# A transformer layer in fp32 on one core: MLP output product in three split passes, heads in fewer transfers

## The reference

```python
qkv_in = rat_read(hidden, read_w ...)            # 3 mixes of width 512, each normalised
attn   = attention(qkv_in, qkv_w, pos)           # causal, rotary, [T, 512]
hidden = rat_write(hidden, attn, wod_w, wab_w ...)
g_in, u_in = split(rat_read(hidden, mlp_read_w ...))
mlp    = silu(g_in @ W0.T) * (u_in @ W1.T)       # [T, 2048]
hidden = rat_write(hidden, mlp, wod_w, wab_w ...)
x = x + hidden
x = x + ffn(layernorm(x))                        # router over 8 low-rank experts

def rat_write(res, y, ...):
    o_d = y @ wod_w.T                            # 512 columns out, 8 of "delta_low"
    A_B = y @ wab_w.T + wab_b                    # 112 columns of gates
    delta = softplus(delta_low @ du_w.T + du_b)
    ...                                          # A_full, B_full: elementwise from delta and the gates
    return hs * A_full + out * B_full
```

## Time and profile before

| | us |
|---|---|
| median of 3 runs | 1699.76 (1698.36 to 1703.68) |
| the profiled execution | 1699.55 |
| its span, first to last instruction | 1697.7 |
| TensorE busy | 1552.1 (91%) |
| VectorE busy | 1157.3 (68%) |
| ScalarE busy | 840.9 (50%) |
| GpSimd busy | 525.1 (31%) |
| DMA moved | 366.45 MB, mean 216 GB/s |

### The profile page before, as it was taken

How to read it: one execution, slowest core, us unless ns; L and a number is a source line. 1 busy time by engine, 2 the same in 40 slices (tenths; PEclk the granted TensorE clock), 3 DMA queues, 4 the chain that set the end, 5 groups by cost and what they waited for, 6 DMA issues and landing times.

```text
span 1697.7 us, 22468 instructions
## 1 busy us (share of the span) xinstructions
PE 1552.1 (91%) x8278; PEld 1052.8 (62%) x8278; DVE 1157.3 (68%) x1686; ACT 840.9 (50%) x1528; POOL 525.1 (31%) x430
## 2 busy tenths in 40 slices
PE   6999999999999977599998899988899989999976
PEld 5665555666666645577655677555677557876544
DVE  7777755888888857644458668767767874354775
ACT  5233235888888755444234456234465325442352
POOL 1424533333331000225563641452551352000000
PEclk9999999999999988699999999999999999999987
DMA  9657567888786155367675577766677766676743
GB/s 359 210 196 303 183 172 223 237 220 240 212 233 178 46 195 162 132 205 247 218 267 186 189 258 278 244 219 203 234 250 259 263 209 194 222 247 215 233 157 136
DMA packets 126273, 366.45 MB, mean 216 GB/s; under 512 B 16066, under 2 KB 33090, under 8 KB 110932
## 3 DMA queue, kind: packets, MB, share of 16 engines
q1 hardware_dynamic: 125876, 364.88, 66.1%
q10 hardware_dynamic: 288, 0.13, 0.0%
HBM read 289.20 MB, written 75.76 MB: 215 GB/s over the span
## 4 chain that ended last, share of the span: by engine, by line
PE 69%; DVE 17%; ACT 8%; issue 3%; DMA 2%; POOL 1%; SPq 0%; DVEq 0%; ACTq 0%
PE ps L1574 20%; PE ps L1586 11%; PE ps L545 6%; PE ps L1038 5%; PE ps L1025 4%; PE ps L1061 4%; PE ps L1544 3%; PE ps L1532 3%; ACT a_p L1140 3%; PE ps L1489 2%; DVE m_A L1644 2%; PE ps L504 2%; PE ps L1473 2%; PE ps L1504 1%; DMA p_x<-in_x 1%
## 5 line engine op out<-in xcount | busy, mean ns | idle before, releaser
L1574 PE MATMUL ps<-m_yhi,m_win 128*128 128x512 f32 x1024 | 355.9, 416 | 0.0
L1586 PE MATMUL ps<-m_wod,m_hT 128*128 128x512 f32 (+1 forms) x1024 | 296.8, 440 | 4.4 <-DVE m_mlp_ab L1779 2.5
L1586 PEld LDWEIGHTS ps<-m_wod,m_hT 128*128 128x128 f32 x1024 | 167.2, 194 | 147.1 <-issue 145.0
L1574 PEld LDWEIGHTS ps<-m_yhi,m_win 128*128 128x128 f32 x1024 | 195.1, 190 | 53.2 <-issue 8.2
L1082 DVE TENSOR_REDUCE a_negmax<-ps 128x1 f32<-128x640 f32 (+7 forms) x176 | 180.8, 1027 | 60.6 <-PE ps L1028 59.6
L1574 PE MATMUL ps<-m_ylo,m_win 128*128 128x512 f32 x512 | 204.0, 398 | 0.0
L1140 ACT ACTIVATE a_p<-ps,a_negmax 128x128 f32<-128x128 f32 (+7 forms) x256 | 188.8, 751 | 28.6 <-DVE a_negmax L1082 26.3
L1038 PE MATMUL ps<-ident,a_p 128*128 128x128 f32 x1152 | 156.7, 274 | 1.4 <-DVE a_pT L1095 1.2
L1964 POOL TENSOR_SCALAR e_moments<-e_moments 128x1 f32<-128x1 f32 x16 | 7.4, 463 | 431.5 <-ACT m_x L1875 401.5
L1025 PE MATMUL ps<-a_k,a_q 128*128 128x512 f32 (+3 forms) x384 | 123.5, 401 | 16.9 <-ACT a_p L1140 15.0
L1038 PEld LDWEIGHTS ps<-ident,a_p 128*128 128x128 f32 x1152 | 122.9, 141 | 3.3 <-DVE a_pT L1095 1.9
(11 more groups left out here) (218 smaller groups left out, 2808.9 us busy)
## 6 DMA issues: line engine op xcount, KB each, us to landing
m_win<-mlp_in_split SPq DMA_DIRECT2D x128, 512.0 KB, 4.5
m_wod<-in_wod2T SPq DMA_DIRECT2D x128, 316.0 KB, 3.4
m_wod<-in_wod1T SPq DMA_DIRECT2D x64, 316.0 KB, 3.6
p_xT<-in_xT SPq DMA_DIRECT2D x16, 1024.0 KB, 9.3
p_x<-in_x SPq DMA_DIRECT2D x16, 1024.0 KB, 10.6
a_q<-qk_split SPq DMA_DIRECT2D x64, 256.0 KB, 6.9
a_k<-qk_split SPq DMA_DIRECT2D x128, 128.0 KB, 7.1
mlp_in_split<-a_w_two SPq DMA_DIRECT2D x32, 512.0 KB, 3.5
```

Source lines behind the costliest of these rows:

```text
L1574: m = nc.tensor.matmul(bank_of("m", blk, step), win[s][:, wl, ic, :], y[:, k, :], start=(ic == 0 and p3 == 0), stop=(ic == HCH - 1 and p3 ...
L1586: m = nc.tensor.matmul(ps[:, b, 0:cn], hT[:, k, P * q:P * q + P], w2[s][:, c0:c0 + cn], start=(k == 0), stop=(k == MCH - 1))
```

## The change

1. Blocks 0 to 2 make the MLP output in fp32r, as the input products are made. The 632 columns are cut into two halves of 316 (`HALFW`); a half now covers all four tiles, with three products per tile and step: high x high, high x low, low x high. Each tile has one bank per half. Block 3 stays as it was, in fp32, two tiles per half.
2. `hT` is split on the chip: an entry `h` per chunk (16 per block), placed at steps 30.2 to 38.8, copies it into the high part on ScalarE and subtracts on VectorE for the low part. The high part uses the buffer of `yhi` and `ylo`; the next block's turns wait until the step that read it is done.
3. The MLP output weights are split by GpSimd beside attention: 32 more pieces of 316 columns; all 64 are spread evenly over units 0 to 163.
4. The heads: one transfer for q and two for k, each to two groups of partitions, instead of two and four; and one head per unit in units 2 to 5 instead of four in unit 3.
5. `PLACES` has new numbers throughout. The writes of a block's tiles, two of which began in the middle of the block, begin after it (w0 at 64 instead of 48). Buffers of the last four tiles are named anew.

```diff
+SPLIT = [blk < NBLK - 1 for blk in range(NBLK)]
+ROUNDS = [[(0, 1, 2, 3)] * 2 if SPLIT[blk] else [(0, 1), (2, 3)] for blk in range(NBLK)]
+HALFW = (H + 8 + 2 * 48 + 16) // 2
 PLACES = {...
-'A': 'loado': -3.11, 'wod': 1.56, 'low': 2, 'load': 3.17, 'delta': 4, 'gates': 5.65, 'scale': 7.94, 'sum': 9.57,
-     'piece0': 13.67, 'piece1': 13.68, 'piece2': 14.32, 'piece3': 14.5, 'stats': 18.05, 'norm': 20.16
+'A': 'loado': -1.0, 'wod': 1.09, 'low': 2.18, 'load': 4.08, 'delta': 4.24, 'gates': 6.17, 'scale': 8.72, 'sum': 9.72,
+     'piece0': 14.75, 'piece1': 14.76, 'piece2': 14.77, 'piece3': 16.73, 'stats': 18.62, 'norm': 20.12
-'FIRST': 'wod': 2.03, 'low': 3.03, 'delta': 4.35, 'gates': 5.03, 'scale': 6.03, 'sum': 7.29, ...
+'FIRST': 'wod': 0.95, 'low': 1.95, 'delta': 2.95, 'gates': 3.79, 'scale': 3.8, 'sum': 5.46, ...
-'a': 4: 0.0, 5: 12.0, 6: 24.0, 7: 36.05, 8: 50.7, 9: 66.7, 10: 81.09, 11: 98.7, 12: 114.7, ...
+'a': 4: -4.73, 5: 9.49, 6: 22.54, 7: 36.68, 8: 54.57, 9: 68.62, 10: 83.01, 11: 94.12, 12: 118.84, ...
-'w': 0: 48, 1: 64, 2: 81.06, 3: 96.37, 4: 112, 5: 127.33, 6: 144, 7: 160, 8: 176, 9: 192, 10: 208, 11: 224, ...
+'w': 0: 64, 1: 78.28, 2: 90.67, 3: 103.13, 4: 128.04, 5: 140, 6: 155, 7: 167.9, 8: 192.26, 9: 204, 10: 218.0, ...
-'t': first of block 1 62.25, of block 2 120.61, of block 3 185.15
+'t': first of block 1 56.81, of block 2 120.9, of block 3 183.25
+'h': 30.22, 30.72, 30.94, 31.22, 31.44, 32.5, 32.72, 32.73, 33.64, 33.73, 34.44, 35.24, 35.4, 37.1, 38.03, 38.83
...
+        placed += [(64 * blk + at, ("h", blk, "split", m)) for blk in range(NBLK) if SPLIT[blk]
+                   for m, at in enumerate(PLACES["h"])]
...
+            if SPLIT[blk]:
+                pe.wait_ge(hlo_ready, MCH * sum(SPLIT[:blk]) + k + 1)
+                for q in tiles:
+                    if k == 0:
+                        wait_for_bank(pe, "d", blk, q, r)
+                    for p3, (h, wl) in enumerate(((Y, 0), (Y, 1), (hT_lo, 0))):
+                        m = nc.tensor.matmul(bank_of("d", blk, q, r)[:, 0:HALFW], h[:, k, P * q:P * q + P],
+                                             w2s[s][:, wl, :], start=(k == 0 and p3 == 0),
+                                             stop=(k == MCH - 1 and p3 == 2))
...
+        def split_dve(blk, m):
+            dve.wait_ge(hhi_ready, MCH * sum(SPLIT[:blk]) + m + 1)
+            V.tensor_tensor(hT_lo[:, m, :], hT[:, m, :], Y[:, m, :].bitcast(F32), ALU.subtract).then_inc(hlo_ready, 1)
+        def split_act(blk, m):
+            act.wait_ge(mlp_mm, 32 * blk + (30 if m < MCH // 2 else 32))
+            wait_for_emptied(act, "m", blk, up_step(m))
+            S.activation(Y[:, m, :], hT[:, m, :], ACT.Copy).then_inc(hhi_ready, 1)
...
+            if blk and SPLIT[blk - 1]:
+                act.wait_ge(wod2_mm, wod2_done(blk - 1, 1, 2 * k + 1))
             wait_for_emptied(act, "t", blk, k)
+            S.activation(yhi[k], yraw[k % 2][:, :], ACT.Copy).then_inc(yhi_ready, 1)
...
+                for q in ROUNDS[blk][r]:
+                    act.wait_ge(wod2_mm, wod2_count[blk, r, k, q])
+                    act.wait_ge(hs_ready, nth("sum", *before_place(blk, q)))
...
+        PIECES = 4 * MCH
+        def pieces_at(n):
+            return [u for u in range(PIECES) if n == u * (NU - 10) // PIECES]
...
-            for r in range(2):
-                move(qs[s][64 * r:64 * r + 64, :], src_q).then_inc(slot_loaded[s], 16)
-            for r in range(4):
-                move(ks[s][32 * r:32 * r + 32, :], src_k[r // 2]).then_inc(slot_loaded[s], 16)
+            move(qs[s][:, :], src_q.unsqueeze(0).broadcast_to([2, 64, L])).then_inc(slot_loaded[s], 16)
+            for a in range(2):
+                move(ks[s][64 * a:64 * a + 64, :], src_k[a].unsqueeze(0).broadcast_to([2, 32, L])).then_inc(slot_loaded[s], 16)
...
-                if n < NU and si % 3 == 0 and u == 3 and sets[si][0] + 1 < fours:
+                if n < NU and si % 3 == 0 and u in (2, 3, 4, 5) and sets[si][0] + 1 < fours:
```

More of the change, by code:

```diff
@@ L47 @@
 ACT_SET = "natural_log_exp_and_others"
[L52 to L102, removed]
@@ new lines @@
+PLACES = {'A': {'loado': -1.0,
+       'wod': 1.09,
+       'low': 2.18,
+       'load': 4.08,
+       'delta': 4.24,
+       'gates': 6.17,
+       'scale': 8.72,
+       'sum': 9.72,
+       'piece0': 14.75,
+       'piece1': 14.76,
+       'piece2': 14.77,
+       'piece3': 16.73,
+       'stats': 18.62,
+       'norm': 20.12},
+ 'W': {'load': -0.7, 'low': 0, 'delta': 1.6, 'gates': 2.49, 'loadx': 3.3, 'scale': 3.87, 'sum': 5.21, 'x': 6.46},
+ 'E': {'mean': 8.55,
+       'turn0': 9.73,
+       'turn1': 10.69,
+       'spread': 12.86,
+       'down0': 13.14,
+       'turn2': 13.64,
+       'down1': 13.74,
+       'turn3': 14.21,
+       'down2': 15.46,
+       'down3': 15.58,
+       'router': 15.75,
+       'weigh': 16.93,
+       'lowT': 19.44,
+       'out0': 20.6,
+       'out1': 21.13,
+       'out2': 23.66,
+       'out3': 23.67,
+       'store': 23.68},
+ 'FIRST': {'loado': -102.01,
+           'load': -100.37,
+           'wod': 0.95,
+           'low': 1.95,
+           'delta': 2.95,
+           'gates': 3.79,
+           'scale': 3.8,
+           'sum': 5.46,
+           'turn0': 6.98,
+           'turn1': 6.99,
+           'turn2': 7.9,
+           'turn3': 7.91,
+           'read0': 8.59,
+           'read1': 8.6,
+           'read2': 10.8,
+           'read3': 10.81,
+           'stats': 11.86,
+           'norm': 13.35},
@@ L105 @@
        2: -194,
[L106 to L130, removed]
-       12: 240,
[L132 to L154, removed]
+       3: -191,
+       4: -4.73,
+       5: 9.49,
+       6: 22.54,
+       7: 36.68,
+       8: 54.57,
+       9: 68.62,
+       10: 83.01,
+       11: 94.12,
+       12: 118.84,
+       13: 132,
+       14: 145.3,
+       15: 159.5},
+ 'w': {0: 64,
+       1: 78.28,
+       2: 90.67,
+       3: 103.13,
+       4: 128.04,
+       5: 140,
+       6: 155,
+       7: 167.9,
+       8: 192.26,
+       9: 204,
+       10: 218.0,
+       11: 230.85,
+       12: 240,
+       13: 243.3,
+       14: 255.91,
+       15: 259.19},
+ 'e': {0: 64,
+       1: 78.48,
+       2: 91,
+       3: 103.35,
+       4: 129.61,
+       5: 143.11,
+       6: 155,
+       7: 171.01,
+       8: 192,
+       9: 203.89,
+       10: 223.5,
+       11: 231.08,
+       12: 239.56,
+       13: 245.5,
+       14: 254.71,
+       15: 260.67},
+ 't': [-2.97, -2.73, -2.49, -2.25, -2.01, -1.76, -1.52, -1.28, 56.81, 57.86, 58.91, 59.96, 61.01, 62.06, 63.11, 64.17,
+       120.9, 121.98, 123.05, 124.13, 125.2, 126.28, 127.36, 128.43, 183.25, 184.42, 185.59, 186.77, 187.94, 189.11,
+       190.29, 191.46],
+ 's': 36.83,
+ 'h': [30.22, 30.72, 30.94, 31.22, 31.44, 32.5, 32.72, 32.73, 33.64, 33.73, 34.44, 35.24, 35.4, 37.1, 38.03, 38.83]}
 class Engine:
@@ L1387, in program @@
             if what == "m" and part >= 32 and (part - 32) % MCH == 0:
-                for b in range(4):
-                    one.plan(("d", i, (part - 32) // MCH, b), b)
+                r = (part - 32) // MCH
+                for q2 in ROUNDS[i][r]:
+                    if SPLIT[i]:
+                        one.plan(("d", i, q2, r), q2, readers=1 + r)
+                    else:
+                        one.plan(("d", i, q2, 0), 2 * (q2 % 2))
+                        one.plan(("d", i, q2, 1), 2 * (q2 % 2) + 1)
             if what == "m" and (i, part) == (NBLK - 1, 63):
@@ L1793, in mix_dve @@
                     turn_dve(i, q)
+                elif what == "h":
+                    split_dve(i, q)
                 else:
```

150 lines of the change are left out of this document (94 added, 56 removed).

## The result

The changed kernel takes 2280.32 us (median of 4 runs, 2276.01 to 2283.72) against 1699.3 of the kernel before on the same chip: a ratio of 1.341 [1.338, 1.345]. 1666 us were predicted, 1640 to 1694 as the range. The prediction was wrong, in sign and by 614 us.

What follows compares the result with a forecast made beforehand. The prediction took TensorE (69% of the chain, the two MLP products longest), idling mostly for VectorE, as the bound. Terms -37+6+3-2-3 = -33 took the profiled 1699.55 us to 1666 us, range 1640 to 1694.

Steps and rivals of the forecast that it cites:

- Heads in 3 transfers: Attention stage: same bytes in 3 transfers instead of 6, no TensorE instruction waits there for a DMA: 0.
- 64 slices, one head at a time: Attention stage: GpSimd's pieces double to 64; heads are fetched early and backlog made up later: 0 (up to +33).
- Order of the mix stage: Writes, reads and turns around the MLP blocks: moved places priced only within small terms, part of +6, +3, -2, -3.
- +6: Blocks 1 and 2: subtractions raise VectorE to 82% busy, adding 3 us of TensorE idling to each (0 to +25).
- +3: Turn before block 1: TensorE waits 13 us on the late last attention write, in exchange for 11 us idled now.
- Output product with its splits: Blocks 0 to 2: 316-column products every 0.148 us, 1.78 us a step instead of 2.16: -37 us (bounds -73, +12).
- the rival of the weight loads: Output product: weight loads of 0.19 us set the pace of the narrow products; 1715 us, chance 0.06.
- VectorE takes over, 1684: Blocks 1 and 2: VectorE sustains no more than 78%, blocks take 251 and 232 us, +17 to +30; chance 0.14.
- Block 0: Block 1's first L1574 near 912 instead of 937: -12 products, -3 start, about 10 us of writes and experts leaving.
- The first writes: First four writes, before block 0: new order puts tile 0's scale ahead of the wait for tile 1's product: -3.
- The tail: After the last product: order much the same with two tiles a little earlier: -2 (-6 to +3).
- DMA engines: Attention: engines don't exceed a 0.84 share, so L1025 waits for a_q or a_k: +33, 1699 us, chance 0.05.

Runs made afterwards that it cites:

- after_heads6: Changed kernel with only the heads' transfers put back (q in two, k in four), still one head per unit: 1760.02 us, ratio 1.036.
- before_slices64: Kernel before with 64 weight slices split and stored instead of 32, the further 32 unused: 1727.25 us, ratio 1.015.
- heads6_group: Changed kernel with the heads in six transfers and all four heads of a group loaded in one unit: 1769.10 us, ratio 1.040.
- before_neworder: Kernel before with only the changed kernel's written order of the mix stage (PLACES, lanes of the last writes): 1750.16 us, ratio 1.028.
- GpSimd short: GpSimd's read mix on 16 of 512 columns: kernel before 1661.94 us; with new order 1660.89; changed kernel with heads in six transfers 1648.50.
- heads6_nosplit: Changed kernel with heads in six transfers and the output product as before (fp32, halves of two tiles, no subtractions): 1767.79 us, ratio 1.040.
- six: Same kernel as after_heads6: the changed kernel with the old six transfers per head: 1760.02 us, ratio 1.036.

## Why the prediction was wrong, step by step

| Step | Forecast | Measured | From |
|---|---|---|---|
| Heads in 3 transfers | 0 | +520 | after_heads6 |
| 64 slices, one head at a time | 0 (up to +33) | +18 (27 - 9) | before_slices64, heads6_group |
| Order of the mix stage | part of +6, +3, -2, -3 | +50 | before_neworder |
| Output product with its splits | -37, and the rest of +6 | -8 (edge of the noise); -31 with GpSimd short | heads6_nosplit, the table above |

1700 + 50 + 18 - 8 = 1760, what six takes; + 520 = 2280.

**Heads.** The step that failed is "the same bytes in 3 transfers instead of 6; no instruction of TensorE waits there for a DMA, so 0". The bytes were the same; the engines that carry them were not. I counted bytes and issues and never asked how a transfer is dealt out. The diff has `broadcast_to([2, 64, L])` as the outermost dimension; the attention stage of before has its transfers at 0.84 of 16 engines, with 1 MB a head and some 11 us of TensorE a head (337/32). At 229 GB/s a head takes 4.6 us. At an eighth of that rate it would be 37; the two engines moved 26 GB/s each instead of some 15, which makes it 20. Neither can hide behind 11. "No wait now" covers a transfer only as long as its duration stays.

**The product.** Forecast 0.144 to 0.152 us between starts. The changed kernel (TensorE, start, us; three products per 0.44 us):

```profile
1369.22 0.46 PE L1638 MATMUL ps<-m_wods,m_y_split 128*128 128x316 f32 x2
1369.51 0.31 PE L1638 MATMUL ps<-m_wods,m_hT_lo 128*128 128x316 f32 x1
1369.66 0.46 PE L1638 MATMUL ps<-m_wods,m_y_split 128*128 128x316 f32 x2
```

0.147 us: the term was sized right on TensorE, and the rival of the weight loads is out. Most of it didn't arrive in the time because TensorE was no longer what set the pace: with GpSimd short the same product is worth 31 us. The estimate by the Trainium skill's formula (TensorE: Matmul & The Clock Gate, "Back-to-back issue gap"), 134 ns, is further from this row than the slope was; the section gives it for a single product in isolation, and here every product has its weight load.

**VectorE.** The step that failed is "+6 (0 to +25)" for VectorE, together with the small terms of the order. The subtractions were forecast at 14 us a block (11 to 20) beside GpSimd, and took 51.0 in the three blocks of six, 17 each. A nearly right count of the added work hid the larger one: I priced VectorE's load as mean busy share (82%) where the new order crowds four tiles into 40 steps, and forgot that GpSimd's work is crowded with it, which stretches VectorE's old instructions. Rows 9 and 10 had that price (1.76 to 3.12 us), and I used it only for what was new. The rival "VectorE takes over, 1684" had the place and the mechanism, at less than half the price: +17 to +30 over the forecast's 241 and 225 us for blocks 1 and 2, where six takes 280 and 264, +78. Its busy share was right (78% forecast, 77 and 80% measured); its work was not: 216 and 210 us of VectorE in these blocks instead of 196 and 181, because the old instructions took longer. The Trainium skill's rule on two SBUF inputs (SBUF — State Buffer, "Who interferes with whom") agrees with the groups above. The same section puts `tensor_scalar` among the operations that can take the shared ports, when its operands meet certain conditions; L1646 at 0.18 and 1.25 us fits that, as one pair of instructions.

**Block 0** was forecast at about 196 us (22 less than 218: 12 of products, 10 of writes and experts that leave it) and takes 199 to 200. That this is near is luck: with the new order and the old product it takes 197 (before_neworder) and 196 (heads6_nosplit). All of the gain is the order's; the product's 12 don't show. The turn before block 1 waits 2 us for the normalisation, not 10; instead L1551 waits 13 us for VectorE in that block.

**The edges.** The first writes: -3 forecast, +4 measured (626.3 to 740.9 in six, 609.2 to 719.4 before); TensorE waits 8.7 us for a weight there, 7.1 before, so that wait explains little of it. Block 3: nothing forecast, +8 (208.5 against 200.9), for work shifted into it, while TensorE is busy throughout. The tail: -2 forecast, -13 (63.0 against 75.6). The last two probably come of one shift of work into block 3; no run shows it.

**Attention.** The bound of +33 for twice the slices held (+27). The rival "DMA engines", to which I gave 0.05, forecast this: a share that stays near 0.84 and a wait for keys, and both are in the trace (0.85; 17.3 us). Whether the engines' share or SyncE's queue is the cause stays open, but for the 9 us of the order of loading.

## What to carry to other kernels

Before a transfer is costed by its bytes, read the outermost dimension of its source: with 2 and 4 entries only 2 and 4 of the 16 engines carried it, and joining transfers by a leading broadcast of 2 made a head 4.4 times as slow (20 us against 4.6). Keep the separate transfers; a broadcast that isn't outermost was not run. When a schedule crowds one engine's work, crowd its neighbours' in your sum too, and price old instructions at the stretched duration and not only the added ones. A faster product is worth its saving only in the stretches where its engine ends last after the change.

## What the runs showed of the hardware that I had not expected

- A DMA with a first dimension of 2, 4 and 16 on its source moved 52 GB/s, 104 GB/s, and as fast as separate transfers (245 GB/s, among other transfers): 26 GB/s an engine with 2 and 4, and 16 an engine with 16.
- Issuing such a DMA of keys (256 KB) held SyncE for 4.9 us in the median with 2 (up to 17.7), 2.4 with 4 and 0.6 with 16; an issue of 128 KB before took 0.4.
- GpSimd's 14 tensor operations a tile cost the kernel before 39 us of 1701 (1661.94 with 16 of their 512 columns), although GpSimd is 1% of the chain that ended last.
- A small VectorE operation on 128x48 went from 0.18 to 1.25 us beside GpSimd, a larger factor than that of a wide one (1.76 to 3.11).
